# The modulated layer after an LSTM: computed behind the recurrence, or within its loop

## The reference

```
def lstm(x, h0, Wx, Wh, b):                    # Wx, Wh: [256, 1024]
    a = x_t @ Wx + b + h @ Wh                  # 1024 times, one after the other
    i, f, o, g = sigmoid, sigmoid, sigmoid, tanh of the quarters of a
    c = f * c + i * g;  h = o * tanh(c)
x = x + lstm(x, cond, Wx, Wh, b)
ys = cond / sqrt(256)
d = rsqrt((ys * ys) @ (weight * weight) + 1e-8)
x = x + ((x * ys) @ weight) * d
```

## Time and profile before

| | |
|---|---|
| median of 3 runs | 1780.48 us (1779.52 to 1782.09) |
| profiled execution, as a run | 1782.03 us |
| its span, first to last instruction | 1780.2 us |
| PE matmul / weight load busy | 94% / 90% |
| ACT / DVE / POOL busy | 62% / 56% / 15% |

### The profile page before, as it was taken

One profiled execution on the slowest core, in us unless ns is written; L12 is line 12 of the kernel. 1 busy time (PEld: TensorE's weight loads), 2 busy tenths in 40 slices (PEclk: granted clock), 3 DMA queues, 4 the chain that ended last, 5 costly groups with the idle time before them and its releaser, 6 DMA issues.

```text
span 1780.2 us, 355694 instructions
## 1 busy us (share of the span) xinstructions
PE 1666.3 (94%) x164108; PEld 1608.2 (90%) x164108; DVE 1002.0 (56%) x7455; ACT 1098.2 (62%) x8196; POOL 259.4 (15%) x1293
## 2 busy tenths in 40 slices
PE   7999999999999999999999999999999999999998
PEld 6999999999999999999999999999999999999996
DVE  2555555555555555555555555555555555555554
ACT  2666666666666666666666666666666666666663
POOL 0111111111111111111111111111111111111110
PEclk7999999999999999999999999999999999999999
DMA  2000000000000000000000000000000000000001
GB/s 84 19 0 0 0 0 0 0 0 0 0 0 0 0 0 0 0 0 0 0 0 0 0 0 0 0 0 0 0 0 0 0 0 0 0 0 0 0 0 47
DMA packets 4585, 6.69 MB, mean 4 GB/s; under 512 B 1248, under 2 KB 3040, under 8 KB 4576
## 3 DMA queue, kind: packets, MB, share of 16 engines
q1 hardware_dynamic: 3872, 5.51, 0.9%
q10 hardware_dynamic: 704, 1.05, 0.2%
HBM read 4.46 MB, written 2.10 MB: 4 GB/s over the span
## 4 chain that ended last, share of the span: by engine, by line
PE 82%; DVE 12%; ACT 3%; issue 3%; DMA 0%; SPq 0%; POOL 0%; DVEq 0%
PE pG L227 35%; PE pX L209 19%; PE pH L227 14%; PE pS L227 14%; DVE pH L371 4%; DVE pH L347 4%; ACT fgate L185 3%; DVE hst L378 2%; DVE parts L366 2%; DVE pG L343 1%; PE pG L308 1%; DMA xh<-in_xT_dram 0%; PE pS L299 0%; DVE ores L395 0%; SPq L114 0%
## 5 line engine op out<-in xcount | busy, mean ns | idle before, releaser
L227 PE MATMUL pG<-hst,wh_sb 128*32 128x16 f32 x65536 | 1082.9, 187 | 98.0 <-DVE hst L378 88.0
L227 PEld LDWEIGHTS pG<-hst,wh_sb 128*32 128x32 f32 x65536 | 942.5, 109 | 148.3 <-DVE hst L378 112.8
L185 ACT ACTIVATE fgate<-pH 128x2 f32<-128x2 f32 x2048 | 354.8, 173 | 600.1 <-PE pH L227 599.8
L227 PE MATMUL pH<-hst,wh_sb 128*32 128x16 f32 x32768 | 673.5, 185 | 3.2 <-issue 3.2
L366 DVE TENSOR_TENSOR parts<-fgate,pH 128x2 f32<-128x2 f32 x2048 | 319.9, 156 | 583.1 <-ACT fgate L185 582.9
L227 PEld LDWEIGHTS pH<-hst,wh_sb 128*32 128x32 f32 x32768 | 589.2, 110 | 1.8 <-issue 1.8
L227 PE MATMUL pS<-hst,wh_sb 128*32 128x16 f32 x32768 | 506.6, 186 | 4.1 <-issue 4.1
L209 PE MATMUL pX<-xp,wx_sb 128*32 128x8 f32 x32896 | 459.4, 181 | 2.7 <-issue 1.6
L227 PEld LDWEIGHTS pS<-hst,wh_sb 128*32 128x32 f32 x32768 | 424.3, 108 | 4.3 <-issue 4.3
L146 POOL TENSOR_TENSOR xh<-xh,hst 128x4 f32 (+1 forms) x1024 | 208.7, 204 | 1491.5 <-DVE hst L378 1491.5
L371 DVE TENSOR_TENSOR_SCAN pH<-parts 128x6 f32<-128x6 f32 x2048 | 367.1, 179 | 82.7 <-ACT parts L187 0.7
(11 more groups left out here) (41 smaller groups left out, 99.8 us busy)
## 6 DMA issues: line engine op xcount, KB each, us to landing
outT_dram<-ores SPq DMA_DIRECT2D x8, 256.0 KB, 2.5
xh<-in_xT_dram SPq DMA_DIRECT2D x6, 320.0 KB
wh_sb<-in_Wh_dram ACTq DMA_DIRECT2D x1, 1024.0 KB, 8.0
wx_sb<-in_Wx_dram SPq DMA_DIRECT2D x1, 1024.0 KB, 7.5
w_sb<-in_w_dram SPq DMA_DIRECT2D x1, 256.0 KB, 7.0
xh<-in_xT_dram SPq DMA_DIRECT2D x2, 64.0 KB, 8.0
condT<-in_condT_dram ACTq DMA_DIRECT2D x1, 2.0 KB, 7.7
bias_col<-in_bC_dram ACTq DMA_DIRECT2D x1, 3.0 KB, 7.4
```

Of the source, the lines that this page charges most:

```text
L185: act.activation(fgate[:, j, :], forgets[j][:, cols], ACT.Sigmoid).then_inc(fgate_ready[j], 1)
L227: last = pe.matmul(to[c * Q:(c + 1) * Q, :], tile(wh_sb[:, k, :], c, j, g), hst[:, k, WIDE * t:WIDE * (t + 1)], start=False, stop=True, sk ...
```

## The change

The layer moves into the loop, two bodies behind the recurrence. In body `it` GpSimd multiplies the body's four outputs (x + h) by yscale into `xm`, with the spread ahead of it. PE sums `xm` against the plain weights one body later: 4 of its 16 matmuls behind the x sums of step 1, 12 behind those of step 2. In the body after, DVE scales these sums by `demod` into `res` behind the second product of step 0, and GpSimd adds the matching columns of `xh`. `demod` is formed before the loop: the weights are loaded first by GpSimd's queue, squared before the second spread, summed by PE before the first x sums, rooted by ACT before its table for Sigmoid is loaded. `xh` and `res` have 2T columns more in front. The output goes out in three cuts: after 512 steps, after 960, and at the end, two DMAs each. PE's fillers write to `pX`, and `pL` takes the place of `pF`.

```diff
-    NOUT = 512
-    NCH = SEQ // NOUT
+    X0 = 2 * T
...
-        xh = sb("xh", [P, K, B, SEQ + 2 * T])
+        xh = sb("xh", [P, K, B, X0 + SEQ + 2 * T])
+        xm = sb("xm", [P, K, ROWS])
+        res = sb("res", [P, K, B, X0 + SEQ])
...
-        wmod = sb("wmod", [P, B, K, D])
-        ores = sb("ores", [P, 2, NOUT])
...
-        pF = ctx.enter_context(nc.psum_tensor("pF", [P, 512], F32))
+        pL = ctx.enter_context(nc.psum_tensor("pL", [P, 512], F32))
...
+        layer = pL[:, 0:K * ROWS]
+        squared = pL[:, K * ROWS:K * (ROWS + B)]
...
+        OUTCUT = [0, 512, 960, SEQ]
...
-            sp.dma_start(w_sb[:, :, :], w.rearrange("(k p) o -> p k o", p=P)).then_inc(w_loaded, 16)
...
+            for lo, hi in zip(OUTCUT, OUTCUT[1:]):
+                sp.wait_ge(result_ready, hi // T + 2)
+                for o in range(K):
+                    sp.dma_start(outT[o * P:(o + 1) * P, :, lo:hi], res[:, o, :, X0 + lo:X0 + hi]).then_inc(out_written, 16)
...
+            pool.dma_start(w_sb[:, :, :], w.rearrange("(k p) o -> p k o", p=P)).then_inc(w_loaded, 16)
+            pool.memset(xh[:, :, :, 0:X0], 0.0)
+            pool.memset(xm[:, :, :], 0.0).then_inc(xm_ready, 1)
...
+            def add_x(n):
+                cols = bass.ds(n * T, T) if not isinstance(n, int) else slice(n * T, (n + 1) * T)
+                pool.tensor_tensor(res[:, :, :, cols], res[:, :, :, cols], xh[:, :, :, cols], ALU.add).then_inc(result_ready, 1)
...
+            spread(slice(X0, X0 + T))
+            pool.wait_ge(w_loaded, 16)
+            pool.tensor_tensor(wsq[:, :, :], w_sb[:, :, :], w_sb[:, :, :], ALU.mult).then_inc(squares_ready, 1)
...
+                    pool.wait_ge(xh_ready, it * T + 2 * T)
+                    pool.wait_ge(layer_summed, it + 2)
+                    pool.wait_ge(layer_scaled, it + 1)
                     pool.wait_ge(x_summed, it + 2)
-                    spread(bass.ds(it * T + 2 * T, T))
-                    if aside is not None:
-                        aside()
...
+                    spread(bass.ds(it * T + (X0 + 2 * T), T))
+                    pool.tensor_tensor(xm[:, :, :].rearrange("p k (b t) -> p k b t", b=B), xh[:, :, :, bass.ds(it * T + X0, T)],
+                                       yscale[:, :, :].unsqueeze(3).broadcast_to([P, K, B, T]), ALU.mult).then_inc(xm_ready, 1)
+                    add_x(it)
...
-            for k in range(K):
-                bodies(EARLY + k, EARLY + k + 1, lambda: squares(k))
-            for n in range(B * K):
-                bodies(EARLY + K + n, EARLY + K + n + 1, lambda: modulated(n // K, n % K))
-            bodies(EARLY + K + B * K, NBODY)
+            bodies(EARLY, NBODY)
+            for n in (NBODY, NBODY + 1):
+                pool.wait_ge(layer_scaled, n + 1)
+                add_x(n)
...
-            act.activation(warmed[:, :], zeros[:, 0:1], ACT.Sigmoid)
+            act.activation(warmed[:, 0:1], zeros[:, 0:1], ACT.Sqrt)
+            act.wait_ge(demod_added, 1)
+            act.activation(demod[:, :, :], demod[:, :, :], ACT.Sqrt).then_inc(demod_rooted, 1)
+            act.activation(warmed[:, 1:2], zeros[:, 0:1], ACT.Sigmoid)
...
+            LAYER = [(o, k) for o in range(K) for k in range(K)]
+
+            def sum_layer(groups):
+                for o, k in groups:
+                    for c in range(G):
+                        lo = o * P + c * Q
+                        last = pe.matmul(layer[c * Q:(c + 1) * Q, o * ROWS:(o + 1) * ROWS], w_sb[:, k, lo:lo + Q], xm[:, k, :],
+                                         start=(o == 0 and k == 0), stop=True, skip_group_check=True)
+                return last
...
+            pe.wait_ge(squares_ready, 1)
+            pe.wait_ge(ysq_ready, 1)
+            for o in range(K):
+                for k in range(K):
+                    for c in range(G):
+                        lo = o * P + c * Q
+                        last = pe.matmul(squared[c * Q:(c + 1) * Q, o * B:(o + 1) * B], wsq[:, k, lo:lo + Q], ysq[:, k, :],
+                                         start=(o == 0 and k == 0), stop=True, skip_group_check=True)
+            last.then_inc(demod_summed, 1)
 
             pe.wait_ge(operands_ready, 2)
             pe.wait_ge(xp_ready, 1)
...
                     elif s == 1:
                         sum_x_cells(1)
+                        pe.wait_ge(layer_scaled, it + 1)
+                        pe.wait_ge(xm_ready, it + 1)
+                        sum_layer(LAYER[:1])
                     elif s == 2:
                         sum_x_outs().then_inc(x_summed, 1)
+                        sum_layer(LAYER[1:]).then_inc(layer_summed, 1)
...
+            pe.wait_ge(layer_scaled, NBODY + 1)
+            pe.wait_ge(xm_ready, NBODY + 1)
+            sum_layer(LAYER).then_inc(layer_summed, 1)
...
+            def scale_layer(n):
+                cols = bass.ds(n * T, T) if not isinstance(n, int) else slice(n * T, (n + 1) * T)
+                dve.wait_ge(layer_summed, n + 1)
+                dve.tensor_tensor(res[:, :, :, cols], layer.rearrange("p (o b t) -> p o b t", o=K, b=B),
+                                  demod[:, :, :].unsqueeze(3).broadcast_to([P, K, B, T]), ALU.mult).then_inc(layer_scaled, 1)
...
                     if s == T - 1:
                         carry_outs()
...
+                    elif s == 0:
+                        scale_layer(it)
+
+            for n in (NBODY, NBODY + 1):
+                scale_layer(n)
```

More of the change, by code:

```diff
@@ L75, in build @@
         xouts = pX[:, K * NG * ROWS:K * (NG + 1) * ROWS].rearrange("p (j r) -> p j r", r=ROWS)
-        pD, pO = pS[:, 0, :], [pG[:, j, :] for j in range(K)]
+        layer = pL[:, 0:K * ROWS]
+        squared = pL[:, K * ROWS:K * (ROWS + B)]
         x_begun, x_loaded, cond_loaded, w_loaded, wx_loaded, wh_loaded, bias_loaded = (sem(n) for n in (
             "x_begun", "x_loaded", "cond_loaded", "w_loaded", "wx_loaded", "wh_loaded", "bias_loaded"))
-        out_written = [sem(f"out_written{n}") for n in range(2)]
+        out_written = sem("out_written")
         buffers_zeroed, operands_ready = (sem(n) for n in ("buffers_zeroed", "operands_ready"))
[L82 to L85, removed]
+        ys_ready, ysq_ready, squares_ready, demod_summed, demod_added, demod_rooted, demod_ready = (sem(n) for n in (
+            "ys_ready", "ysq_ready", "squares_ready", "demod_summed", "demod_added", "demod_rooted", "demod_ready"))
+        picks_zeroed, xp_ready, x_summed, zeros_ready, xh_ready = (sem(n) for n in (
+            "picks_zeroed", "xp_ready", "x_summed", "zeros_ready", "xh_ready"))
+        xm_ready, layer_summed, layer_scaled, result_ready = (sem(n) for n in (
+            "xm_ready", "layer_summed", "layer_scaled", "result_ready"))
         sums_ready = [sem(f"sums_ready{j}") for j in range(K)]
@@ L117, in _ @@
                 for k in range(K):
-                    sp.dma_start(xh[:, k, :, lo:hi], xT_in[k * P:(k + 1) * P, :, lo:hi]).then_inc(x_loaded, 16)
-            sp.dma_start(w_sb[:, :, :], w.rearrange("(k p) o -> p k o", p=P)).then_inc(w_loaded, 16)
[L121 to L125, removed]
+                    sp.dma_start(xh[:, k, :, X0 + lo:X0 + hi], xT_in[k * P:(k + 1) * P, :, lo:hi]).then_inc(x_loaded, 16)
@@ L134, in _, with bodies @@
             pool.wait_ge(x_begun, 16 * K)
-            spread(slice(0, T))
+            spread(slice(X0, X0 + T))
+            pool.wait_ge(w_loaded, 16)
+            pool.tensor_tensor(wsq[:, :, :], w_sb[:, :, :], w_sb[:, :, :], ALU.mult).then_inc(squares_ready, 1)
             pool.wait_ge(x_summed, 1)
-            spread(slice(T, 2 * T))
-            def bodies(lo, hi, aside=None):
+            spread(slice(X0 + T, X0 + 2 * T))
+            pool.wait_ge(ys_ready, 1)
+            def bodies(lo, hi):
@@ L235, in clear @@
                 for c in range(G):
-                    pe.matmul(of[c * Q:(c + 1) * Q, :], picks[:, :], zeros[:, 0:of.shape[1]], start=True, stop=True)
+                    last = pe.matmul(of[c * Q:(c + 1) * Q, :], picks[:, :], zeros[:, 0:of.shape[1]], start=True, stop=True)
+                return last
[6 more added lines that the diff above has]
+                                         start=(o == 0 and k == 0), stop=True, skip_group_check=True)
+                return last
             def filler(count, start=False):
                 for _ in range(count):
-                    pe.matmul(pF[0:Q, 0:P], picks[:, :], zeros[:, :], start=start, stop=True, skip_group_check=True)
+                    pe.matmul(pX[0:Q, 256:256 + P], picks[:, :], zeros[:, :], start=start, stop=True, skip_group_check=True)
             pe.wait_ge(zeros_ready, 1)
```

57 lines of the change are left out of this document (12 added, 45 removed).

## The result

The changed kernel takes 1822.05 us (median of 4 runs, 1821.27 to 1823.88) against 1780.15 us of the kernel before on the same chip: a ratio of 1.0235, interval 1.0217 to 1.0253. Its profiled execution has a span of 1822.1 us, 41.9 us more than before. The forecast was 1794.5 us with a range up to 1818: the sign was right, the size was not.

A forecast was written before the change was run, and what follows sets the result against it. PE was taken to wait for the recurrence at every step, with small slack; 1780.2 + 23 (loop) - 12.6 (tail) + 3.9 (start) + 0.5 (output DMAs) - 0.8 (asides) = 1794.2, median 0.3 higher: 1794.5 us, range 1770 to 1818.

The forecast's parts named there:

- PE's waits in step 1: PE's waits for layer_scaled and xm_ready in the loop's second step, both met over 1 us ahead: 0.01 us.
- Layer pairs behind s = 1: 8 layer pairs on PE in the second step: 0.08 us added, 0.03 slack, so 0.05 us late.
- Layer pairs behind s = 2: 24 layer pairs on PE in the third step: 0.24 us added, 0.19 slack, so 0.05 us late.
- The hole that is given back: A late PE step no longer waits for the second product, returning about 0.02 us in each late step.
- GpSimd ahead of the spread: New GpSimd waits make the spread's copy 0.40 us late, step 0's x sum 0.04: +0.02 us per body net.
- The start: Before and in the loop's first pass: weight load, squares, more code and lower clock add 3.9 us (1 to 7).
- The tail: After the last product the end comes sooner, at 1767.6 us: -12.6 us (-11 to -13.5).
- The asides: The old wsq and wmod operations leave six bodies, where they lengthened VectorE scans: -0.8 us.
- The output DMAs in the loop: Output DMAs within the loop add 0.5 us.
- A: Rival: late PE catches up in the next step, the loop stays at 1.69 us per step: 1771.5 us, chance 0.22.
- B: Rival: without the wait PE's fast first part is lost in late steps, 0.24 us per body: 1833 us, chance 0.08.
- C: Rival: GpSimd's xm and add_x lengthen VectorE's scans in step 0, +31 us: 1825 us, chance 0.12.

The follow-up runs named there:

- The last experiment: Changed kernel with spread first, PE's two waits ahead of s = 2's x sums, all layer matmuls behind them in bfloat16 (16 pairs): 1771.53 us against 1780.65.

## Why the prediction failed, point by point

Two steps of the sum failed, about equally dear: PE's waits, and the hole that late steps were to give back. The loop's term was +23 us and came to 53.5, 30 short: 20 are the waits, 15 the hole, and 5 are taken off again by two terms that were put too high.

- *PE's waits in step 1, taken at 0.01 us:* they cost 0.087 us in the changed kernel and 0.073 in the kernel before. "Met long before" was true and beside the point: of two waits in a row one is an instruction of its own in PE's stream, and only 8 pairs follow in which a hole could be won back. The bound, "between zero and one register operation each", did cover it, up to twice 0.051 us. A row was there to choose by: the kernel before has two waits in a row behind its loop (lines 302 and 303), and its trace has the same instruction of 51 ns at line 303.
- *Layer pairs behind s = 1:* 10 ns per pair and 0.03 us of slack gave 0.05; 0.042 was measured without waits, 0.041 in the changed kernel with the waits elsewhere. Right.
- *Layer pairs behind s = 2:* 0.24 less 0.19 gave 0.05; 0.048. Right. The last experiment, whose 16 pairs fit into this slack and cost nothing, bears it out.
- *The hole that is given back, -0.02 in each late step:* the wait was read rightly, and it does go, but nothing comes of it. Before, the load that reads the second product starts 0.26 us behind the step's first (904.28, 904.54):

```profile
904.54 0.16 PEld L227 LDWEIGHTS pH<-hst,wh_sb 128*32 128x32 f32 x7
...
904.61 0.22 PEld L227 LDWEIGHTS pG<-hst,wh_sb 128*32 128x32 f32 x14
```

In the late step of the changed kernel it starts 0.24 us behind (905.04, 905.28):

```profile
905.28 0.18 PEld L232 LDWEIGHTS pH<-hst,wh_sb 128*32 128x32 f32 x7
...
905.37 0.22 PEld L232 LDWEIGHTS pG<-hst,wh_sb 128*32 128x32 f32 x14
```

The row of 14 starts 0.33 us behind the first load in both. Means over 190 bodies say the same: the 33rd load of the late step comes 0.020 us earlier, the 41st and all later ones no earlier, and from a step's first load to its product it takes 1.48 us before and in this late step. Behind the hole the next 8 loads take 0.063 us, without it 0.083: before the change PE had won the hole back at once, so there was nothing to return. In the late steps behind s = 0 and s = 2 a step even takes 0.007 us more. So each of the three returns of 0.02 that the prediction took off is missing, 0.06 us per body. What paces the loads behind the hole, no run shows.

- *GpSimd ahead of the spread:* the copy starts 0.58 us after the add instead of 0.18, 0.40 late as worked out; the x pairs start 0.20 us before the product (902.77, 902.97) instead of 0.30, 0.10 late as worked out; the interval grows by 0.030, where 0.04 was taken. Right, and its removal takes 0.028 away. The return of 0.02 that went with it did not come, as above.
- *The start* (+3.9 taken): the first product is 4.4 us later. The x sums start at 13.51 us instead of 10.65, behind squares of 1.14 us, and take 1.83 instead of 1.18 us. They run wholly at the lower clock level (0.50 granted, 1.2 GHz), where before they had 1.00: the granted clock fell at 11.25 us, in a stretch of 4.23 us in which PE stood idle behind its fillers; before, it fell at 15.54 us. The first pass of the loop is then 1.5 us shorter, not longer. Net 2.9, where 3.9 was taken: an under- and an overestimate that partly cancel, and so in part luck. The first pass lasts 16.9 to 18.1 us in all kernels with the layer in the loop and 18.9 to 20.6 in those without; why was not tried.

```profile
11.92 1.14 POOL L145 TENSOR_TENSOR wsq<-w_sb 128x512 f32<-128x512 f32 x1
...
13.11 0.52 PEld L274 LDWEIGHTS pL<-ysq,wsq 128*32 128x32 f32 x32 [4.23 <-POOL wsq L145]
...
13.51 1.83 PEld L214 LDWEIGHTS pX<-xp,wx_sb 128*32 128x32 f32 x128
```

The granted clock is the third number from the end in the view of busy time by stretch, here that of the x sums:

```profile
13.51:15.34 1.83, 1.83 (x144) 1.82 (x138) 0.16 (x1) 1.35 (x2) 0.00 (x0) 0.50 0.00 0
```

- *The tail* (-12.6): -13.4. Its last links, from GpSimd's xm to the last sums, scaling and addition, take 1.4 us to the DMA:

```profile
1817.67 0.21 POOL L163 TENSOR_TENSOR xm<-xh,yscale 128x16 f32<-128x16 f32 x1
...
1818.00 0.38 PEld L250 LDWEIGHTS pL<-xm,w_sb 128*32 128x32 f32 x32 [1.95 <-issue]
...
1818.53 0.17 DVE L388 TENSOR_TENSOR res<-pL,demod 128x16 f32<-128x16 f32 x1 [1.64 <-PE pL L250]
1818.79 0.22 POOL L140 TENSOR_TENSOR res<-res,xh 128x16 f32<-128x16 f32 x1 [0.55 <-DVE res L388]
```

- *The small terms.* The asides (-0.8): the six bodies of before are 0.11 us longer each, so -0.7. The output DMAs in the loop (+0.5): the two bodies beside them last 7.47 and 7.50 us instead of 6.98, so +1.0; it lies in the means above.
- *The rivals.* A (absorbed) did not happen. With half the pairs the time is A's 1771.5, but not by A's way: there nothing is late, so nothing is caught up. B (the pace is lost) came nearest by its total, 1833, but is not the mechanism: a late step's first 16 loads take 0.23 us, as in the late step of before, and the late steps have no 0.07 of their own. C is real and small here, about 1 us over the run; it is a matter of where the operations fall, 10 us in the kernel with the spread first.

## What to carry to other kernels

Measure the slack of each shadow by the overlap of its last load with the next step's first, against a step that is late: that gave two slacks within 0.01 us, and said how much work fits (behind s = 2 16 pairs did, at no cost, 32 did not). Never put two waits in a row just ahead of the last few instructions of a saturated stream, however long they have been met: put them apart, put them ahead of a long stretch, or let another engine's wait cover one; here that is 17 to 20 of 42 us. And a gap that is a true wait need not be worth its length: where a long enough stretch follows it is won back, so count on it only when the loads well behind it come earlier in a step that lacks it.

## What was not expected of the hardware

- Two met waits in a row in PE's stream cost 0.073 us ahead of 8 pairs, one costs 0.000 (1.735 us with and without it), two apart none either. One of a row of two is an instruction of 51 ns of its own; a single wait leaves none.
- A VectorE scan over 6 elements takes 0.24 us instead of 0.18 when a GpSimd operation of 16 elements per partition starts with it (249 of 256 bodies), though that operation is only 0.22 us long; when it starts some 10 ns behind the scan, it is the one that takes 0.24. Before the change this showed only beside operations of 256 elements.
- fp32 pairs of a load of 32 columns and 8 moving columns come about every 10 ns at the end of a step, whether they sum x, the layer or nothing (x48 in 0.57 us, x32 in 0.41, pL x24 in 0.32 above).
- PE wins small holes in its stream back: the 0.02 us of waiting for a step's second product within 8 loads, the 0.035 us of two waits in a row within 30. So they cost nothing in mid-stream and all at the end, and closing one in mid-stream gains nothing.
